# Graph-attention layer on one core: turning the normalized rows by a DMA instead of by TensorE

## The reference

```python
h = jnp.maximum(_layernorm(x, axis=-1), 0.0)
q = split_heads(h @ Wq.T); k = split_heads(h @ Wk.T); v = split_heads(h @ Wv.T)   # 16 heads of 32
a = jnp.einsum('bhnd,bhmd->bhnm', q, k) * 512 ** -0.5 + (adj + adj)[:, None]
a = jnp.where(jnp.any(a != 0, axis=-1, keepdims=True), a, -jnp.inf)
p = jax.nn.softmax(a, axis=-1)                       # rows without any entry give 0
o = jnp.einsum('bhnm,bhmd->bhnd', p, v)              # heads joined again
out = x + o @ Wo.T
```

## Time and profile before

| quantity | value |
|---|---|
| median of 3 runs | 1005.16 us |
| the profiled execution's own time | 1005.16 us |
| its span, first to last instruction | 1003.4 us |
| mean granted TensorE clock | 0.989 |
| busy in the span: PE, ACT, POOL, DVE | 959.6, 934.5, 862.3, 850.0 us |
| mean busy share of the DMA engines | 9 tenths or more from the third slice on |

### The profile page before, as it was taken

How to read it: one execution, slowest core, us unless ns; L and a number is a source line. 1 busy time by engine, 2 the same in 40 slices (tenths; PEclk the granted TensorE clock), 3 DMA queues, 4 the chain that set the end, 5 groups by cost and what they waited for, 6 DMA issues and landing times.

```text
span 1003.4 us, 33752 instructions
## 1 busy us (share of the span) xinstructions
PE 959.6 (96%) x11580; PEld 660.2 (66%) x11580; DVE 850.0 (85%) x3092; ACT 934.5 (93%) x3049; POOL 862.3 (86%) x936
## 2 busy tenths in 40 slices
PE   5879999999999999999999999999999999999965
PEld 4656776666677666777666677766666776667632
DVE  6778998888989888898988889988889898888863
ACT  5799999999999999999999999999999999999992
POOL 2278998989998898999888899989889988889894
PEclk9989999999999999999999999999999999999979
DMA  6289999999999999999999999999999999999995
GB/s 251 49 148 195 183 190 194 183 193 186 190 191 184 195 178 187 194 199 180 192 177 198 183 203 184 189 194 178 198 183 197 186 191 193 177 185 176 175 175 119
DMA packets 573818, 183.62 MB, mean 183 GB/s; under 512 B 547024, under 2 KB 555216, under 8 KB 573648
## 3 DMA queue, kind: packets, MB, share of 16 engines
q1 hardware_dynamic: 573648, 181.48, 100.9%
...
## 4 chain that ended last, share of the span: by engine, by line
PE 56%; DVE 28%; issue 8%; ACT 5%; POOL 1%; DMA 1%; DVEq 0%; POOLq 0%; ACTq 0%; SPq 0%
PE ps L1045 35%; DVE logits L752 15%; PE ps L1113 9%; PE ps L1063 7%; DVE stats L649 4%; ACT probs L547 3%; PE ps L942 3%; DVE q_lo L815 2%; DVE o_norm L782 2%; PE ps L1089 1%; DVE some L770 1%; ACT p L560 1%; PE ps L1019 1%; DMA w_nat<-in_L_gnn_Wq 1%; DVE row_min L752 1%
## 5 line engine op out<-in xcount | busy, mean ns | idle before, releaser
L430 POOL TENSOR_TENSOR p<-probs,p 128x512 f16<-128x512 f32 x512 | 586.4, 1161 | 89.9 <-ACT p L560 89.7
L547 ACT ACTIVATE probs<-logits,row_min 128x256 f32<-128x256 f32 x1024 | 513.6, 511 | 3.8 <-DVE row_min L752 3.8
L752 DVE CUSTOM_DVE_ANT_0 logits<-ps,adj_s,sigma 128x256 f32<-128x256 f32 x1024 | 438.0, 475 | 7.1 <-PE ps L1063 7.0
L560 ACT ACTIVATE p<-probs 128x512 f16<-128x512 f32 x512 | 323.5, 632 | 0.0
L1045 PE MATMUL ps<-ht_hi,w_hi 128*128 128x256 f16 x1024 | 280.2, 274 | 7.7 <-DVE q_lo L815 2.6
L1045 PE MATMUL ps<-ht_lo,w_hi 128*128 128x256 f16 x1024 | 279.4, 273 | 0.0
L1045 PE MATMUL ps<-ht_hi,w_lo 128*128 128x256 f16 x1024 | 279.4, 273 | 0.0
L547 ACT ACTIVATION_READ_ACCUMULATOR probs<-logits,row_min 128x1 f32 x1024 | 209.8, 205 | 0.0
L1045 PE MATMUL ps<-wo,o_hi 128*128 128x512 f16 x496 | 149.2, 383 | 3.8 <-POOL o_lo L456 3.8
L1045 PEld LDWEIGHTS ps<-ht_hi,w_hi 128*128 128x128 f16 x1024 | 100.1, 98 | 36.1 <-DVE q_lo L815 13.0
L1045 PEld LDWEIGHTS ps<-ht_lo,w_hi 128*128 128x128 f16 x1024 | 100.4, 98 | 14.0
...
## 6 DMA issues: line engine op xcount, KB each, us to landing
...
pt<-p SPq DMA_TRANSPOSE x256, 4.0
w_nat<-p SPq DMA_TRANSPOSE x256, 3.4
...
```

Source lines behind the costliest of these rows:

```text
L430: g.tensor_tensor(p16[:, c % 2, k, 1], probs[:, h % 4].rearrange("p u n -> p (u n)"), p16[:, c % 2, k, 0], ALU.subtract).then_inc(p_split, 1)
L547: e = a.activation(probs[:, h % 4, u, :], logits[:, h % 4, u, :], ACT.Exp, bias=row_min[:, t.par(d), u, h:h + 1], scale=-1.0, accum_out=ro ...
L560: a.activation(p16[:, c % 2, k, 0], probs[:, h % 4].rearrange("p u n -> p (u n)"), ACT.Copy)\
L752: v.tensor_tensor_reduce(out=logits[:, h % 4, u, :], in0=ps[:, S_BANK + h % HC, N * u:N * u + N], in1=adj_s[:, t.par(d), u, :], scale=sigm ...
```

## The change

From batch 3 on PE no longer turns the normalized rows. ReLU and the split into `hi` and `lo` are done in SBUF, before the turn, on the untransposed `xn`: for row block 0 ACT writes `hi` at step 5 and DVE `lo` at step 6; for row block 1 DVE writes both at step 10. The result `h16` (128 x 2 x 1024 float16) lies in a part of `w_nat` that the weights no longer use, and is turned by one DMA transpose, issued by SP at step 11 into a new tile `ht` that takes the place of `ht_hi` and `ht_lo`. PE's first q job waits for that transfer. For batches 0 to 2 PE still turns. The scaled variance moves from DVE to POOL, and the negated mean goes away, since `xn` is now made by a subtraction. The tile `ht` is laid out by row block, so that the matmuls read it in two pieces.

```diff
+H_TURNED = 3
+H_BY_ACT = (0,)
+H_HI_STEPS, H_LO_STEPS = (5, 5), (6, 10)
...
+        ht = sb("ht", [P, 2, NU, 2 * NC, P], F16)
...
+        def h_by_dma(b):
+            return b >= H_TURNED
...
         def h_turns(t, s):
             at = (10, 13) if t.first else (5, 8)
-            return [k for k in range(2) if at[k] == s and later(t, 2)]
+            return [k for k in range(2) if at[k] == s and later(t, 2) and not h_by_dma(t.batch(2))]
...
+        def h_parts(t, s, steps):
+            return [u for u in range(NU) if steps[u] == s and later(t, 2) and h_by_dma(t.batch(2))]
+
+        def h_rows_free(eng, b):
+            if b == H_TURNED:
+                eng.wait_ge(wo16_in, 16 * NC)
+            else:
+                eng.wait_ge(ht_in, 16 * (b - H_TURNED))
...
# SP
+                    if s == 11 and later(t, 2) and h_by_dma(t.batch(2)):
+                        b = t.batch(2)
+                        sp.wait_ge(h_split, NU * (b - H_TURNED + 1))
+                        sp.wait_ge(pj_full, NJ * t.batch(0) + 6)
+                        sp.dma_start_transpose(ht[:, b % 2].rearrange("p u l n -> p (u l) n"),
+                                               h16[:, 0:NU].rearrange("p u n -> p (u n)")).then_inc(ht_in, 16)
...
# GpSimd, layernorm
-                pool.wait_ge(ln_stats, NU * (t.batch(d) + 1))
+                pool.wait_ge(stat_step, 2 * NU * (b + 1))
+                g.tensor_scalar(var_s[:], mean_var[:, :, 1], EPS, 2.0 ** (-2 * H_UP), ALU.add, ALU.mult)\
+                 .then_inc(var_ready, 1)
...
# ScalarE
+            def round_h(b, u):
+                act.wait_ge(xn_ready, NU * b + u + 1)
+                h_rows_free(act, b)
+                a.activation(h16[:, u, 0:D], xn[:, u, :], ACT.Relu).then_inc(h_hi_act, 1)
...
# VectorE
-                v.tensor_scalar(neg_mean[:], mean_var[:, :, 0], -1.0, None, ALU.mult).then_inc(ln_stats, 1)
-                v.tensor_scalar(var_s[:], mean_var[:, :, 1], EPS, 2.0 ** (-2 * H_UP), ALU.add, ALU.mult)\
-                 .then_inc(ln_stats, 1)
...
+            def rest_of_h(b, u):
+                n = b - H_TURNED
+                if u in H_BY_ACT:
+                    dve.wait_ge(h_hi_act, len(H_BY_ACT) * n + H_BY_ACT.index(u) + 1)
+                else:
+                    dve.wait_ge(xn_ready, NU * b + u + 1)
+                    h_rows_free(dve, b)
+                    v.tensor_scalar(h16[:, u, 0:D], xn[:, u, :], 0.0, None, ALU.max).then_inc(h_hi_dve, 1)
+                    dve.wait_ge(h_hi_dve, (NU - len(H_BY_ACT)) * n + u - len(H_BY_ACT) + 1)
+                v.scalar_tensor_tensor(out=h16[:, u, D:2 * D], in0=xn[:, u, :], scalar=0.0,
+                                       in1=h16[:, u, 0:D], op0=ALU.max, op1=ALU.subtract).then_inc(h_split, 1)
...
# TensorE, project
-                    if j == 0:
+                    if j == 0 and h_by_dma(t.batch(1)):
+                        pe.wait_ge(ht_in, 16 * (t.batch(1) - H_TURNED + 1))
+                    elif j == 0:
                         pe.wait_ge(aux_taken, aux_after("h", t.batch(1), 1))
```

More of the change, by code:

```diff
@@ L93, in emit @@
         w16 = w_nat.bitcast(F16)
+        h16 = w16[:, 2]
         w_max = sb("w_max", [P, 4])
@@ L111, in emit @@
         mean_var = sb("mean_var", [P, NU, 2])
-        neg_mean = sb("neg_mean", [P, NU])
         var_s = sb("var_s", [P, NU])
@@ L172, in emit @@
         stat_step = sem("stat_step")
-        ln_stats = sem("ln_stats")
+        var_ready = sem("var_ready")
+        h_hi_act = sem("h_hi_act")
+        h_hi_dve = sem("h_hi_dve")
+        h_split = sem("h_split")
+        ht_in = sem("ht_in")
         rstd_ready = sem("rstd_ready")
@@ L230, in emit @@
             for at, key in sorted(slot_uses):
+                if key[0] == "h" and h_by_dma(key[1]):
+                    continue
                 if 0 <= key[1] < NB and not (key[0] == "y" and key[2] not in Y_C):
@@ L401, in layernorm @@
             def layernorm(t, d):
-                pool.wait_ge(ln_stats, NU * (t.batch(d) + 1))
+                b = t.batch(d)
+                pool.wait_ge(stat_step, 2 * NU * (b + 1))
+                if h_by_dma(b - 1):
+                    pool.wait_ge(h_split, NU * (b - H_TURNED))
+                g.tensor_scalar(var_s[:], mean_var[:, :, 1], EPS, 2.0 ** (-2 * H_UP), ALU.add, ALU.mult)\
+                 .then_inc(var_ready, 1)
+                pool.wait_ge(var_ready, b + 1)
                 g.tensor_tensor(rstd[:], var_s[:], minus_half[:], ALU.pow).then_inc(rstd_ready, 1)
-                pool.wait_ge(rstd_ready, t.batch(d) + 1)
-                if d == 2:
-                    pool.wait_ge(aux_full, aux_after("h", t.batch(1), 1))
+                pool.wait_ge(rstd_ready, b + 1)
+                if d == 2 and not h_by_dma(b - 1):
+                    pool.wait_ge(aux_full, aux_after("h", b - 1, 1))
                 for u in range(NU):
-                    g.tensor_scalar(xn[:, u, :], xs[:, t.batch(d) % X_RING, u, :], neg_mean[:, u:u + 1],
-                                    rstd[:, u:u + 1], ALU.add, ALU.mult).then_inc(xn_ready, 1)
+                    g.tensor_scalar(xn[:, u, :], xs[:, b % X_RING, u, :], mean_var[:, u, 0:1],
+                                    rstd[:, u:u + 1], ALU.subtract, ALU.mult).then_inc(xn_ready, 1)
             layernorm(first, 1)
@@ L630, in slot @@
                         take_h(t.batch(2), k)
+                    for u in h_parts(t, s, H_HI_STEPS):
+                        if u in H_BY_ACT:
+                            round_h(t.batch(2), u)
             run(act, slot)
@@ L652, in ln_mean_var @@
                 step = 2 * NU * t.batch(d)
+                need(dve, xn_ready, NU * t.batch(d))
                 for u in range(NU):
@@ L722, in take_h @@
                 dve.wait_ge(aux_hi, 2 * b + (k + 1))
-                two = ps[:, bank, :].rearrange("p (c n) -> p c n", c=2)
-                v.scalar_tensor_tensor(out=ht_lo[:, b % 2, 2 * k:2 * k + 2, :], in0=two, scalar=0.0,
-                                       in1=ht_hi[:, b % 2, 2 * k:2 * k + 2, :],
+                v.scalar_tensor_tensor(out=ht[:, b % 2, k, NC:2 * NC, :].rearrange("p c n -> p (c n)"),
+                                       in0=ps[:, bank, :], scalar=0.0,
+                                       in1=ht[:, b % 2, k, 0:NC, :].rearrange("p c n -> p (c n)"),
                                        op0=ALU.max, op1=ALU.subtract).then_inc(aux_taken, 1)
+            def rest_of_h(b, u):
+                n = b - H_TURNED
+                if u in H_BY_ACT:
+                    dve.wait_ge(h_hi_act, len(H_BY_ACT) * n + H_BY_ACT.index(u) + 1)
[6 more added lines that the diff above has]
+                                       in1=h16[:, u, 0:D], op0=ALU.max, op1=ALU.subtract).then_inc(h_split, 1)
             for u in range(NU):
@@ L862, in slot @@
                             take_h(t.batch(2), k)
+                        for u in h_parts(t, s, H_LO_STEPS):
+                            rest_of_h(t.batch(2), u)
                     for b, u in residuals(t, s):
@@ L939, in turn_h @@
                     need(pe, aux_taken, aux_before("h", b, k))
-                for c in range(2):
-                    for u in range(NU):
-                        m = tr(ps[:, bank, N * c + P * u:N * c + P * u + P],
-                               xn[:, u, P * (2 * k + c):P * (2 * k + c) + P], ident[:])
+                for c in range(NC):
+                    m = tr(ps[:, bank, P * c:P * c + P], xn[:, k, P * c:P * c + P], ident[:])
                 m.then_inc(aux_full, 1)
@@ L982, in _ @@
             W = (w_hi, w_lo)
-            HT = (ht_hi, ht_lo)
             O = (o_hi, o_lo)
```

10 lines of the change are left out of this document (3 added, 7 removed).

## The result

| kernel | median, us (range, runs) | against before |
|---|---|---|
| before | 1005.13 (1004.38 to 1005.19, 4) | |
| after | 1089.87 (1087.51 to 1090.39, 4) | 1.0843 [1.0827, 1.0859] |

The changed kernel is 85 us slower; the forecast was 1028 us, with an upper end of 1048. Its lines are renumbered: `xn` is made at L447 (before L410), POOL's `rstd` at L441, `p`'s rest at L467 (L430), ACT's rounding of row block 0 at L569, DVE's ReLU at L779 and its `lo` at L781, q_lo and k_lo at L871, v_lo at L861, `o_norm` at L838, the projections at L1105; the new transpose is L403.

What follows compares the result with a forecast made beforehand. PE was taken as the bound, with DVE's path to o0 right behind; period 28.91 + w, with w = 1.4, gives 30.3 us, 0.79 over 29.52, times 29 slots is 22.9 us: 1028 us, range 1013 to 1046 (986 to 1048 with rivals).

Steps and rivals of the forecast that it cites:

- What is removed: PE's eight transposes a batch, 0.50 and 0.43 us, and its wait for q_lo; with nothing else, period 28.29 us.
- `q_lo` wait: PE waits 0.30 us for q_lo behind DVE's negated mean and variance; removing those, some 0.58 us, ends it.
- What is added off the path: New work on ACT, DVE and POOL away from o0, and matmuls reading ht in two pieces: costs nothing.
- The DMA: The 512 KB transpose after head 10 lands in 5.25 us; PE wants it after 6.4: hidden by 1.1 us.
- The path to o0 and w: From ACT's taking of k01 over DVE to PE's o0: 9.34 us becomes 9.53 plus w; period 28.91 + w.
- w: What DVE's ReLU and lo of row block 1 wait for POOL: 0.88 plus 0.5, taken as 1.4 us.
- the rest of the period: Slot time outside the path to o0, after removals: 29.52 - 9.34 - 0.30 - 0.50 = 19.38 us.
- the prediction's end of 1043 us: Both of DVE's waits for POOL before o0 whole: w = 1.9, period 30.8 us, +37.5, 1043 us.
- signs of being right: ReLU near 1.3 us or lo near 1.7; PE waiting 1.5 to 2.5 before o0, not for q_lo; period near 30.3.
- Rival 1: DVE's pair mostly falls between POOL's operations: w 0 to 0.5, 987 to 1002 us, typically 995; chance 0.28.
- Rival 3: PE's clock falls because PE idles before o0: 33.9 us a slot, 1132 us; chance 0.05.
- Rival 4: The ht transfer lands, say, 1.1 us too late for PE's first q job: 1060 us; chance 0.04.

Runs made afterwards that it cites:

- e8: The changed kernel with xn by addition, small operations on POOL, and from batch 3 no turn, split or transfer (output wrong): 981.4 us.
- e5: The changed kernel with PE turning all batches, xn by addition, negated mean and variance on POOL, no transfer: 995.8 us, 0.9910 of before.
- e1: The changed kernel with POOL's xn by addition instead of subtraction, mean not negated (output wrong): 1042.5 us.
- e3: The changed kernel with the negated mean again on DVE and xn by addition, output right: 1043.5 us.
- e12: The changed kernel with xn by addition, negated mean on POOL, without DVE's ReLU and lo of row block 1 (output wrong): 1037.5 us.
- e15: The kernel where PE turns all batches (995.8 us) plus a 512 KB transpose at step 8 into a tile nobody reads: 1023.9 us.
- e14: The kernel with no turn or split from batch 3 (981.4 us) plus only the 512 KB transpose at step 8 (output wrong): 1025.3 us.
- e6: The changed kernel with xn by addition, negated mean on POOL, DVE's ReLU and lo of row block 1 at step 8 instead of 10: 1037.1 us.

## Why the prediction was wrong

Right was the direction. By its own steps:

- **What is removed.** PE's 28.29 us for a slot without the turn: e8, which has nothing in its place, took 981.4 us, (981.4 - 1005.2) / 29 + 29.52 = 28.7 us, 0.4 more. ACT, counted at 28.2 us of work, is at 766 of 800 there and waits remain. The `q_lo` wait was sized well: e5 removes it in 31 slots, 0.30 x 31 = 9.3 us, and 8.9 were measured (995.8 for 1004.7 in the same series).
- **What is added off the path: the failed step.** The prediction priced POOL's part by the one new operation of 128 x 2, in 2.6 us of free time, and said "nothing". It did not price the line that had changed its operator. `xn` by subtraction is 2 x 1.31 = 2.6 us more a slot on POOL, exactly what POOL had free, in one block, and this alone is 1089.9 - 1042.5 = 47 us (e1). The `var_s` on POOL took 0.19 us, near the 0.16 of the price. The kernel before had no subtraction in this form, so that price had no row, and should have widened the range upwards. Without it the time is 1042.5 us, inside the range. In the same paragraph DVE's `lo` of row block 0 was called covered; priced at 0.69 us, it took at least 0.90 in e3 and 1.42 in e1, and PE waited for a `k_lo` (7.8 us in all in e3, 8.7 in e1).
- **The DMA.** The landing was priced at 5.25 us, and its median was 5.2. What failed is that it was called hidden by 1.1 us: PE waited for `ht` 21 us between 100 and 900 us in after, and 47 in e12, where it waits for little else. SP needed 3.1 us (median) for this issue, against 1.25 for a head's. And its price for the others was not zero: 28 us (e15) to 44 us (e14).
- **The path to o0 and w.** That the pair would wait for POOL was right, and so was about the size, 1.0 (e3) and 1.3 us (e1) for the forecast 1.4. Wrong were the shares: the ReLU, priced with 0.88 of waiting, mostly had 0.1 to 0.4, and `lo`, priced at a half chance of one wait, waited in every slot. The Trainium skill (SBUF — State Buffer, section Who interferes with whom) says that the two exclude each other for a whole instruction; the 1.38 and 1.52 us at 493.44, of operations that take 0.42 (e6) and 0.69 (after) alone, agree. Wrong was also that the rest of the period would stay at 19.38 us: with w = 1.0 the sum gives 29.9 us, and e3 took 30.9 (e1: 30.2 and 30.9). In e3 the missing 1.0 us a slot is PE's waiting for `q_lo`, `k_lo` and `row_min` (25.4 us in 26 slots), behind a DVE whose other operations got longer as well. So e1 and e3 come near the prediction's end of 1043 us by luck. In after itself w was 0.29 us, since the late POOL shifted everything: the term that decided the forecast was nearly absent from the kernel it was made for. Of the signs of being right, the wait for `q_lo` was gone; the wait of PE at o0 was 1.3 us for at least 1.5, the pair was nowhere near 1.3 or 1.7 us, and the period was 32.3 us for 30.3.
- **The ReLU, priced without a row.** It was taken as 0.42 us, and took that in e6 (median of 0.416); in after it took 0.52.
- **Rivals.** Rival 1 (waits miss) describes after's pair, but at 1090 us and not 995. Rival 3 did not come: the granted clock stayed at 1.00 with waits of 1.4 us, and was 0.99 between 100 and 900 us in e6, where PE waited up to 3.4 us. Rival 4 named the late transfer at 1060; alone it gives 1037 (e12). No rival had POOL as the bound.

The three causes don't add: POOL's subtraction hides the other two, the pair at step 10 hides the transfer (1042.5 to 1037), and the transfer's cost remains wherever it is issued (1028 to 1032). What the removal itself is worth, 24 us (e8), is never reached with the transfer in the slot. Why a whole transpose, or two halves, cost a microsecond a slot while a copy and a single half do not stays open: the amount transposed in a slot and the time on SP's in-order queue both fit.
